# First feed-forward product of a perceiver block: one more pair of row blocks by Strassen's scheme, its quadrants built in lent places

## What is computed

```python
def ternarize(W, threshold):
    absW = jnp.abs(W)
    delta = threshold * jnp.max(absW)
    mask = absW > delta
    n = jnp.maximum(jnp.sum(mask), 1)
    alpha = jnp.sum(jnp.where(mask, absW, 0.0)) / n
    return alpha * jnp.sign(W) * mask
...
h = gelu(x @ ternarize(W1).T + b1)      # x 1024 x 1024, W1 4096 x 1024
y = h @ ternarize(W2).T + b2            # W2 1024 x 4096
y = fp4_activation(y)                   # 4-bit rounding, one scale for all of y
```

## Time and profile before

| | us |
|---|---|
| median of 3 runs | 1366.63 (1365.74 to 1366.86) |
| the profiled execution, its own time | 1365.84 |
| its span, first to last instruction | 1364.0 |
| PE busy | 1320.0 (97%) |
| DVE busy | 868.2 (64%) |
| ACT busy | 486.4 (36%) |
| POOL busy | 2.4 |

### The profile page before, as it was taken

How to read it: one execution, slowest core, us unless ns; L and a number is a source line. 1 busy time by engine, 2 the same in 40 slices (tenths; PEclk the granted TensorE clock), 3 DMA queues, 4 the chain that set the end, 5 groups by cost and what they waited for, 6 DMA issues and landing times.

```text
span 1364.0 us, 17551 instructions
## 1 busy us (share of the span) xinstructions
PE 1320.0 (97%) x6738; PEld 640.3 (47%) x6738; DVE 868.2 (64%) x1470; ACT 486.4 (36%) x751; POOL 2.4 (0%) x10
## 2 busy tenths in 40 slices
PE   6999999999999889999999999999999999999995
PEld 4554646444353344444555555444444444444442
DVE  3232424224231377848899986897999997777974
ACT  1121302112020022127777774112555455444432
POOL 0000000000000000000000000000000000000000
PEclk9999999999999989999999999999999999999997
DMA  9999999999999988606656669464477775222264
GB/s 386 419 421 421 420 421 420 422 420 421 420 423 419 364 307 284 249 27 185 175 150 178 171 199 329 176 227 166 168 261 238 230 264 190 77 77 75 78 182 154
DMA packets 142066, 362.00 MB, mean 265 GB/s; under 512 B 63264, under 2 KB 90016, under 8 KB 115616
## 3 DMA queue, kind: packets, MB, share of 16 engines
q1 hardware_dynamic: 138960, 349.86, 70.0%
q10 hardware_dynamic: 3024, 11.01, 2.0%
HBM read 314.70 MB, written 46.14 MB: 265 GB/s over the span
## 4 chain that ended last, share of the span: by engine, by line
PE 79%; issue 14%; DMA 4%; DVE 2%; ACT 0%; DVEq 0%; POOLq 0%; POOL 0%; ACTq 0%
PE ps L1272 14%; PE ps L1156 13%; PE ps L1428 9%; PE ps L1226 8%; PE ps L1339 8%; PE ps L1046 7%; PE ps L1388 6%; DMA ctxT<-in_ctxT 3%; PE ps L1084 3%; PE ps L1138 2%; PE ps L1066 2%; PE ps L1063 1%; PE ps L1292 1%; DMA x_t<-in_x 1%; PE ps L1100 1%
## 5 line engine op out<-in xcount | busy, mean ns | idle before, releaser
L1477 PE MATMUL ps<-t_half,hl 128*128 128x512 f16 x896 | 193.6, 379 | 0.0
L1156 PE MATMUL ps<-ctx_sb,attnT 128*64 128x512 f32 (+1 forms) x832 | 180.3, 593 | 0.0
L780 ACT ACTIVATE stg<-ps 128x512 f32<-128x512 f32 (+1 forms) x66 | 36.3, 552 | 297.7 <-PE ps L1066 168.3
L1477 PEld LDWEIGHTS ps<-t_half,hl 128*128 128x128 f16 x896 | 87.7, 98 | 105.7
L1046 PE MATMUL ps<-ctxT,x1T 128*64 128x512 f32 x512 | 115.4, 595 | 2.5 <-DMA ctxT<-in_ctxT 2.4
L956 ACT ACTIVATE hl<-hb,al 128x512 f16<-128x512 f32 x112 | 79.2, 720 | 97.5 <-PE ps L1477 83.7
L1156 PEld LDWEIGHTS ps<-ctx_sb,attnT 128*64 128x64 f32 (+1 forms) x832 | 59.0, 137 | 115.3 <-issue 108.5
L1995 DVE SCALAR_TENSOR_TENSOR hl<-hb,al,hl 128x512 f16<-128x512 f32 x112 | 81.9, 749 | 48.7 <-ACT hl L956 48.5
L1226 PE MATMUL ps<-wv_sb,x2T 128*128 128x512 f32 x256 | 112.6, 598 | 0.0
L1339 PE MATMUL ps<-wo_sb,oT 128*128 128x512 f32 x256 | 111.6, 593 | 0.3 <-ACT oT L862 0.3
L1550 DVE SCALAR_TENSOR_TENSOR x1s<-ps,sw,x1s 128x512 f32<-128x512 f32 x16 | 12.0, 751 | 136.3 <-PE ps L1156 136.3
(11 more groups left out here) (227 smaller groups left out, 1801.1 us busy)
## 6 DMA issues: line engine op xcount, KB each, us to landing
ctxT<-in_ctxT SPq DMA_DIRECT2D x64, 1024.0 KB, 22.1
ctx_sb<-in_ctx SPq DMA_DIRECT2D x32, 2048.0 KB, 27.9
ctx_sb<-in_ctx SPq DMA_DIRECT2D x40, 1024.0 KB, 19.6
w_scan<-in_w1t SPq DMA_DIRECT2D x32, 512.0 KB, 6.3
w_buf<-in_w1t SPq DMA_DIRECT2D x32, 512.0 KB, 3.9
w_scan<-in_w2t SPq DMA_DIRECT2D x32, 512.0 KB, 4.7
w_buf<-in_w2t SPq DMA_DIRECT2D x32, 512.0 KB, 4.8
t_dram<-t_set SPq DMA_DIRECT2D x16, 1024.0 KB, 5.1
```

The lines of the kernel that those rows point to most:

```text
L1156: ins = mm(bank(ea + hf)[C * b:C * b + C, :], attnT[0:w, slots[mt], C * b:C * b + C], ctx_sb[0:w, mt, b, hf * BANK:hf * BANK + BANK], star ...
L1477: ins = mm(bank(b), hl[:, r % RING, n, s * P:s * P + P], t_half[:, r % BRING, :], start=(fresh and k == 0 and n == 0), stop=(k == HK - 1 a ...
```

## The change

K1 goes from 12 to 14: twelve of the sixteen k in Strassen's scheme, in six batches. Its parts:

```diff
-K0, K1 = 2, 12
+K0, K1 = 2, 14
...
-N_LATE = FIRST + 7 * (K1 - K0)
+N_LATE = FIRST + 14 * (BATCHES - 1)
+TERN = (4, 4, 4, 5, 5, 4)
+T_FIRST = [2 + sum(TERN[:i]) for i in range(BATCHES + 1)]
...
-        return FIRST + 8 * ((k - K0) // 2) + 2 * (0, 3, 2, 1)[q] + k % 2
+        return FIRST + 8 * ((k - K0) // 2) + 2 * ((2, 1, 0, 3) if k >= K1 - 2 else (0, 3, 2, 1))[q] + k % 2
...
-                 32, 36, 40, 44, 100, 104, 108, 112)
+                 108, 36, 32, 112, 40, 44, 100, 104)
+        h_tmp = sb("h_tmp", [P, 2, 2, BANK], 24 * KB)
...
+        def hk(q, k):
+
+            return h_tmp[:, q // 3, k % 2, :] if k in (K1 - 2, K1 - 1) and q in (0, 3) else hs(q, k)
```

The quadrants q0 and q3 of the last batch are built in `h_tmp`, which lies over the slots 8 to 15 of the pieces, and go to their own places in `hb` (over factors of x that step m = 6 still reads) only with their gelu, after m = 6. So `kept`, `gelu_kept` and `post` use hk in place of hs. ACT's order, and its new place for one count:

```diff
-                for ab in range(2):
-                    gelu_kept(i, 0, ab)
-                for ab in range(2):
-                    gelu_kept(i, 3, ab)
+                for q in () if last else (0, 3):
+                    for ab in range(2):
+                        gelu_kept(i, q, ab)
                 count2(t0 + 2)
                 for ab in range(2):
                     gelu_kept(i, 2, ab)
+                if TERN[i] > 4:
+                    count2(t0 + 3)
                 for ab in range(2):
                     step_done(i, 6, ab)
                     k = K0 + 2 * i + ab
                     gelu(k, 1, bank(4 * ab + roles(i)[0]))
-            n = 1 + 4 * BATCHES
+                for q in (0, 3) if last else ():
+                    for ab in range(2):
+                        gelu_kept(i, q, ab)
+            n = T_FIRST[BATCHES] - 1
```

DVE does as many ternary2 in batch i as TERN says; the fourth and fifth stand behind the posts:

```diff
             for i in range(BATCHES):
-                t0 = 2 + 4 * i
+                t0 = T_FIRST[i]
                 ternary2(t0)
                 ternary2(t0 + 1)
...
-                ternary2(t0 + 3)
-            for n in range(2 + 4 * BATCHES, WT):
+                for n in range(t0 + 3, T_FIRST[i + 1]):
+                    ternary2(n)
+            for n in range(T_FIRST[BATCHES], WT):
                 ternary2(n)
```

SP's order (`turn_w2(n)` stores the pair before n, when n is even, and loads tile n + 2):

```diff
+            def turn_w2(n):
+                if n % 2 == 0:
+                    store_t2(n // 2 - 1)
+                load_w2(n + 2)
+
             load_w2(3)
+            loaded = 24
             for i in range(BATCHES):
...
+                    if s in (2, 5, 7, 12) and (2, 5, 7, 12).index(s) < TERN[i]:
+                        turn_w2(T_FIRST[i] + (2, 5, 7, 12).index(s))
+                    if s == 13 and TERN[i] > 4:
+                        turn_w2(T_FIRST[i] + 4)
+                    if i < BATCHES - 2 or i == BATCHES - 1 or s < 6:
+                        load_piece(loaded)
+                        loaded += 1
+            for n in range(T_FIRST[BATCHES], WT):
+                turn_w2(n)
```

More of the change, by code:

```diff
@@ L327, in build @@
         ctxT_got = [sem(f"ctxT_got{k}") for k in range(SLOTS)]
-        ctxT_used, apart_got = sem("ctxT_used"), sem("apart_got")
+        ctxT_used = sem("ctxT_used")
         vec = sem("vec")
@@ L457, in load_apart @@
                 for i in range(2):
-                    sp.dma_start(slot((NT - 1, "apart", i)), ctxW_in[NT - 1, 2 + i]).then_inc(apart_got, 16)
+                    sp.dma_start(slot((NT - 1, "apart", i)), ctxW_in[NT - 1, 2 + i]).then_inc(n_in, 16)
                 for i in range(2):
-                    sp.dma_start(tails[i][:, :, :, :], ctxE_in[i]).then_inc(apart_got, 16)
+                    sp.dma_start(tails[i][:, :, :, :], ctxE_in[i]).then_inc(n_in, 16)
             def load_N(q, g, part=None):
@@ L679, in _ @@
                 load_piece(n)
+            def turn_w2(n):
+                if n % 2 == 0:
+                    store_t2(n // 2 - 1)
+                load_w2(n + 2)
             load_w2(3)
+            loaded = 24
             for i in range(BATCHES):
-                n0, t0 = 24 + 14 * i, 2 + 4 * i
                 for s in range(14):
[L684 to L705, removed]
+                    if s in (2, 5, 7, 12) and (2, 5, 7, 12).index(s) < TERN[i]:
[5 more added lines that the diff above has]
+                        loaded += 1
+            assert loaded == len(PIECES)
+            for n in range(T_FIRST[BATCHES], WT):
+                turn_w2(n)
             store_t2(HK - 1)
@@ L806, in put_v @@
                 A(v_all[:, t, hf * BANK:hf * BANK + BANK], bank(2 * (t % 2) + hf), ACT.Copy).then_inc(v_out, 1)
-            act.wait_ge(n_in, 16)
+            act.wait_ge(n_in, 80)
             f = slice(BANK, 2 * BANK)
@@ L823, in _ @@
                 if t == 0:
-                    act.wait_ge(n_in, 32)
+                    act.wait_ge(n_in, 96)
                     relu(2)
@@ L936, in kept @@
                 role = (0, 1)[m]
-                A(hs((0, 3)[m], K0 + 2 * i + ab), bank(4 * ab + roles(i)[role]), ACT.Copy).then_inc(f_copy, 1)
+                A(hk((0, 3)[m], K0 + 2 * i + ab), bank(4 * ab + roles(i)[role]), ACT.Copy).then_inc(f_copy, 1)
             def gelu_kept(i, q, ab):
@@ L941, in gelu_kept @@
                 k = K0 + 2 * i + ab
-                gelu(k, q, hs(q, k))
+                gelu(k, q, hk(q, k))
             def count2(n):
@@ L973, in _ @@
             for i in range(BATCHES):
-                t0 = 2 + 4 * i
+                t0, last = T_FIRST[i], i == BATCHES - 1
                 if i == 1:
@@ L1092, in loaded_energies @@
                     if use[1] == "apart":
-                        pe.wait_ge(apart_got, 64)
+                        pe.wait_ge(n_in, 64)
                     else:
@@ L1644, in row_stats @@
                             V.wait_ge(bn_ready, 2)
-                            V.wait_ge(n_in, 16)
+                            V.wait_ge(n_in, 80)
                             own.done(V.tensor_scalar(tok[:, t, f], tok[:, t, f], bnm[:, 6:7], bnm[:, 7:8], ALU.mult, ALU.add))
@@ L2006, in post @@
                     V.wait_ge(f_post, 8 * i + 5 + ab)
-                to, b, more = {2: (hs(2, k), X, hs(3, k)), 3: (hs(0, k), Z, hs(0, k)), 4: (hs(3, k), X, hs(3, k)),
+                to, b, more = {2: (hs(2, k), X, hk(3, k)), 3: (hk(0, k), Z, hk(0, k)), 4: (hk(3, k), X, hk(3, k)),
                                5: (hs(2, k), W, hs(2, k))}[m]
```

## The result

The changed kernel takes 1367.99 us (median of 20 runs, 1366.63 to 1370.18), the kernel before 1365.66 in 20 runs. The ratio is 1.002, its 95% interval 1.0014 to 1.0026: 2.3 us slower. The profiled execution of the changed kernel took 1368.1 us with a span of 1366.3.

The account below looks back on a forecast made before the run. PE was taken as the bound, running without a gap from 977.52 us. Terms -3.45 + 1.68 + 0.33 + 2.54 = +1.10 us on the median 1366.63 gave 1367.7; 8 in 10 range 1365.4 to 1370.2.

Parts of the forecast that it names:

- The matmuls, -3.45: First product, k 12 and 13: 16 fewer matmuls at 0.216 us each, all on the path, -3.45 us.
- DVE's queue, +4.55: Batches 4 and 5: DVE's posts come late, PE waits 1.68, 0.33 and 2.54 us, together +4.55.
- W2's end, cost 0: Behind the batches: W2's last store leaves round 0 ready near 1152.1, PE comes at 1154.76; 2.6 us of cover.
- ACT, SP, the pieces, `make_s`, the semaphore, 0 each: ACT's extra copies and gelus, SP's later piece loads, wider make_s in odd heads, merged semaphore: each claimed to cost zero.
- A wait's own price: Clock loss behind PE's waits for posts, beyond their length: bounds 0 and +1.6 us, taken as 0.
- the row of 2.20 us: Profile row of a 2.20 us PE wait, read as leaving the clock at 1.00; nearest to the longest wait, 2.54.
- The row of 3.36 us: Profile row of a 3.36 us PE wait: clock 0.64 behind it, 26 matmuls took 4.79 us instead of 3.17.
- Rival C: Step m = 4, last batch: clock falls behind the 2.54 us wait, +1.10 + 1.6 = 1369.3; second fall 1370.9; chance 0.11.
- B: Batches: posts are in time and the matmuls' saving stands, 1363.2 us, faster; chance 0.06.
- D: Second product's start: W2's last loads and store land at their longest, together +3.7, 1370.3 us; chance 0.08.
- E: Batches: posts late in only one of the two batches, 1365.2 to 1365.7 us; chance 0.03.

Follow-up runs that it names:

- 3: Changed kernel with DVE's multiply with a sum left out for tiles 16 to 27: 1361.69 against 1365.35 us, ratio 0.9968.
- 6: Changed kernel with the magnitudes of seven even tiles (14 to 26) summed by ACT in place of DVE: 1362.38 against 1365.61 us, ratio 0.9977.
- 2: Changed kernel with four ternary2 in every batch, two moved behind the last batch: 1369.54 against 1365.35 us, ratio 1.003.
- 4: Changed kernel with DVE's posts moved earlier in its order in the last two batches: 1364.69 against 1365.35 us, ratio 0.9998.
- 5: Changed kernel with posts earlier and ACT's copies of m = 1 ahead of its count, last two batches: 1363.9 against 1365.61 us, ratio 0.9989.
- 11: Changed kernel with the two sum_1 of batches 4 and 5 behind the posts of m = 2 and 3: 1365.89 against 1365.64 us, ratio 1.0001.
- 7: Kernel before with only the merged semaphore and the wider make_s: 1366.2 against 1365.61 us, ratio 1.0007.
- 10: Kernel before with only the merged semaphore and the wider make_s, run a second time: 1364.94 against 1365.7 us, ratio 0.9991.
- 9: Changed kernel unedited, run a third time, against the kernel before: 1367.85 us, ratio 1.0014.

## Why the prediction was right, and where not

*The matmuls, -3.45:* shown by 3 and 6, whose stages are 3.45 us shorter.

*DVE's queue, +4.55:* shown. In the time of the profile before (1.18 less) the three releases of PE came at 1089.63, 1096.86 and 1116.64, against 1089.54, 1096.78 and 1116.59 in the working. Experiments 3 and 6 take the cause away and the waits go; 2, 4, 5 and 11 move DVE's work about, and the waits move where its order says, but for 4, where I left ACT's order out of the working.

*W2's end, cost 0:* right, though the working named the wrong last operand. The last store was issued at 1146.68, less 1.18 that is 1145.5 (1145.6 expected), and the first `high` started at 1151.35. The working took `lower`, 1.5 us after that, as what completes round 0. In experiments 2, 4 and 5 PE waits for the first piece of W2, and starts 2.1 to 2.2 us after that load's issue. Here the load is issued at 1151.33, so by that the piece is there near 1153.5 and the cover is about 2.3 us (an estimate; 2.6 expected).

*ACT, SP, the pieces, `make_s`, the semaphore, 0 each:* PE's list of waits has none of them. 7 and 10 bear out the last two.

*A wait's own price, taken as 0:* **this is the term that was mis-sized.** Its bounds were 0 and +1.6, and I took the lower one, because 2.54 us is nearer to 2.20 than to 3.36. It is neither: 1.69 us in one of the three profiles, 0 in two, and by the totals about 1 us on the mean. Nor could the row of 2.20 us carry the choice. Its window is the wait itself; behind it PE does two short matmuls and is idle for 7.46 us more, and there the clock was down (PE's timeline, then the busy time by stretch):

```profile
473.91 0.38 PE L1205 MATMUL ps<-bnm,cst 128*128 128x2 f32 x2 [2.20 <-DVE bnm L1683]
481.75 1.97 PE L1217 MATMUL ps<-cst,x2s 128*128 128x128 f32 x8 [7.46 <-DVE x2s L1676]
...
474.00:481.75 7.75, 0.29 (x3) 0.21 (x3) 6.33 (x21) 2.35 (x4) 0.00 (x0) 0.64 1.02 407
```

The row of 3.36 us was one draw of several too (last section). The price of about 1 us is nearly all of the difference between the forecast's +1.1 and the measured +2.3. The wait and its fall were seen in profiles; that the fall makes up the 1 us of the totals is inferred. Rival C had place, mechanism and price (1.6), but as a thing that happens always or never; it happens in part of the executions, so half of it belonged in the sum. The page named there, TensorE: Matmul & The Clock Gate of the Trainium skill, "A second HAM failure mode: psum-queue depth-cycling", is right here in its direction, that idling between groups of matmuls can drop the clock; the repeated falls it speaks of did not come, behind the waits of 1.60 us the matmuls kept their 0.216 us in all three profiles.

*Rivals B, D, E:* B is refuted by the waits, D by the store, E by late posts in both batches. The range held the time.

*Where luck helped:* the forecast 1367.7 lies 0.3 us from the measured 1367.99, which is closer than the working deserves. It stood on 1366.63, the median of three runs; over 20 runs the kernel before takes 1365.66. A base 1.0 us too high hid most of a change that was 1.2 us too small.

**Left open.** How often the clock falls behind the 2.36 us was not counted, since only one profile per group shows it; "6 to 7 of 10" is worked out from totals, on the assumption that each fall costs 1.69 us. Nor did anything show what decides it in a given execution.

## What to carry to other kernels

When an edit gives an in-order engine more work, write out its order against the deadlines of the engine that bounds the kernel, a term for each instruction: here that gave each delay to 0.1 us. Include the third engine's order as well, for a copy that stands behind a count can be what the second one waits for. Then price a wait of the matmul engine above its length: 16 matmuls saved (3.45 us) were worth it only once the order or the share of the work kept all waits short.

## What the runs showed of the hardware

The granted clock of TensorE is not reproducible from run to run, at equal code. In the three profiles of the changed kernel the 26 matmuls behind the wait near 444 us took 5.97, 5.97 and 3.14 us. The wait was 3.35 us each time, and 3.17 us is what the group takes at full clock. The third one:

```profile
442.83 3.14 PE L1143 MATMUL ps<-conv_s,prob 128*128 128x130 f32 x26 [3.35 <-DVE conv_s L1616]
```

Over all 14 profiles this one wait cost nothing in three (experiments 4, 9, 11), about 1.6 us in eight, the kernel before among them, and 2.8 us in three. So even 3.35 us of idle did not lower the clock each time, and the single row of the prediction was one outcome of three. The 2.36 us wait cost 1.69 us or nothing; waits of 1.16 to 1.61 us never cost anything visible.

The start of the feed-forward part moves with it: 950.03, 949.55 and 945.17 us in the three profiles of the changed kernel, though 948.71 to 948.86 in all four without the sixth batch. The single totals of the kernel before spread over 3.8 us in the first group of 20 (1363.53 to 1367.3) and from 1362.52 to 1368.26 over all groups. With 11 runs against 19 to 31 the interval was still about 1.2 us to either side, with 20 against 20 it was 0.8 us, so one group of this size can't settle an effect of 1 us. A comparison of stages inside the profiles is far sharper: the four profiles without the sixth batch gave 204.62 us four times.
